# Split index query weights of all heads kept on chip; the reciprocals' table of constants replaced by an immediate

## The reference, cut to what matters

```python
iq = (hidden_states @ idx_wq_w).reshape(b, s, 16, 128)      # index queries, 16 heads
ik = hidden_states @ idx_wk_w                                # index keys, one head
iw = hidden_states @ idx_weights_w * 16 ** (-0.5)
idx_scores = einsum('bqn,bnqk->bqk', iw, relu(einsum('bqnd,bkd->bnqk', iq, ik))) * 128 ** (-0.5)
idx_scores = where(causal, idx_scores, -inf)
_, topk_idx = top_k(idx_scores, 128)
...
scores = (einsum(q_nope, k_nope) + einsum(q_pe, k_pe)) * 192 ** (-0.5)   # 32 heads
attn = softmax(where(mask, scores, -inf))
out = einsum('bhqk,bhkd->bqhd', attn, v).reshape(b, s, 32 * 128) @ o_w
```

## Time and profile before

| | us |
|---|---|
| median of 3 runs | 883.79 |
| lowest and highest | 880.57, 884.02 |
| profiled execution | 884.29 |
| its span on the core | 882.5 |

### The profile page before, as it was taken

How to read it: one execution, slowest core, us unless ns; L and a number is a source line. 1 busy time by engine, 2 the same in 40 slices (tenths; PEclk the granted TensorE clock), 3 DMA queues, 4 the chain that set the end, 5 groups by cost and what they waited for, 6 DMA issues and landing times.

```text
span 882.5 us, 20077 instructions
## 1 busy us (share of the span) xinstructions
PE 792.2 (90%) x7384; PEld 487.0 (55%) x7384; DVE 659.0 (75%) x1557; ACT 583.1 (66%) x1308; POOL 580.6 (66%) x509
## 2 busy tenths in 40 slices
PE   4979989977776998888888999999999999999998
PEld 2545544434443555555554677776766776764443
DVE  6365677889999999999988888888887888851000
ACT  2656789988886887877877677666666676750000
POOL 3175368876795788878877787887788888740000
PEclk9989999999999999999999999999999999999999
DMA  8012211112343776666676567897777677871110
GB/s 258 25 37 72 72 49 48 49 53 64 109 123 98 153 170 164 174 168 159 169 164 151 111 128 141 154 157 147 138 137 152 131 152 153 165 152 34 52 53 29
DMA packets 198483, 104.00 MB, mean 118 GB/s; under 512 B 146417, under 2 KB 172401, under 8 KB 198385
## 3 DMA queue, kind: packets, MB, share of 16 engines
q1 hardware_dynamic: 198384, 102.72, 51.9%
HBM read 36.62 MB, written 6.29 MB: 49 GB/s over the span
## 4 chain that ended last, share of the span: by engine, by line
PE 29%; POOL 26%; DVE 15%; issue 13%; DMA 7%; SPq 6%; ACT 4%; POOLq 0%; DVEq 0%; ACTq 0%
PE psS L779 9%; DMA arena<-arena 6%; DVE m L1182 4%; SPq L457 4%; PE psS L706 3%; DVE bias L1189 3%; POOL arena L1457 3%; POOL arena L1455 3%; POOL arena L1483 3%; PE psT L578 2%; PE psS L535 2%; DVE arena L1242 2%; PE psT L558 2%; POOL arena L1366 2%; POOL arena L1462 2%
## 5 line engine op out<-in xcount | busy, mean ns | idle before, releaser
L706 PE MATMUL psS<-keyT,arena 128*128 128x512 f16 (+3 forms) x1152 | 231.5, 329 | 14.9 <-DVE small L1242 6.6
L810 ACT ACTIVATE arena<-psT 128x512 f16<-128x512 f32 (+4 forms) x328 | 154.6, 503 | 110.7 <-PE psT L763 65.8
L1242 DVE CUSTOM_DVE_ANT_0 arena<-psS,bias 128x512 f32<-128x512 f32 (+7 forms) x256 | 191.4, 751 | 41.3 <-PE psS L706 17.6
L997 ACT ACTIVATE arena<-arena,small 128x512 f32<-128x512 f32 (+7 forms) x256 | 197.4, 774 | 27.7 <-DVE small L1242 21.1
L1048 DVE SCALAR_TENSOR_TENSOR arena<-psT,arena 128x512 f16<-128x512 f32 (+3 forms) x246 | 126.3, 535 | 23.1 <-ACT arena L810 22.8
L706 PEld LDWEIGHTS psS<-keyT,arena 128*128 128x128 f16 x1152 | 92.6, 98 | 81.2 <-issue 20.7
L591 PE MATMUL psS<-ikT,big 128*128 128x512 f16 (+3 forms) x528 | 103.8, 341 | 24.2 <-DVE bias L1133 20.8
L1432 POOL TENSOR_TENSOR bias<-arena,bias 128x768 f32<-128x768 f32 (+2 forms) x48 | 91.3, 1916 | 32.3 <-ACT arena L876 21.4
L763 PE MATMUL psT<-ident,arena 128*128 128x128 f32 x624 | 97.0, 277 | 10.1 <-DVE arena L1048 6.9
L591 PEld LDWEIGHTS psS<-ikT,big 128*128 128x128 f16 x528 | 49.5, 100 | 73.8 <-DVE bias L1133 28.1
L1189 DVE MATCH_REPLACE8 bias<-m,bias 128x768 f32<-128x768 f32 (+4 forms) x112 | 89.9, 809 | 0.0
(11 more groups left out here) (164 smaller groups left out, 1417.0 us busy)
## 6 DMA issues: line engine op xcount, KB each, us to landing
arena<-arena SPq DMA_DIRECT2D x192, 128.0 KB, 2.4
arena<-in_wiq SPq DMA_DIRECT2D x32, 256.0 KB, 2.8
arena<-in_ow SPq DMA_DIRECT2D x16, 512.0 KB, 4.1
arena<-in_qbT SPq DMA_DIRECT2D x16, 256.0 KB, 2.5
wvo_parts<-arena SPq DMA_DIRECT2D x16, 256.0 KB, 2.0
arena<-in_qpe SPq DMA_DIRECT2D x16, 128.0 KB, 3.0
arena<-in_x SPq DMA_DIRECT2D x8, 256.0 KB, 3.2
out<-arena SPq DMA_DIRECT2D x8, 256.0 KB, 2.0
```

Of the source, the lines that this page charges most:

```text
L706: last = mm(bank[:, k:k + w], Q[:, u % 2, h, a, q:q + P], keyT[:, b, h, k:k + w], start=(a, b) == (0, 0), stop=(a, b) == (1, 0))
L810: return nc.scalar.activation(dst, src, ACT.Copy, scale=scale)
L997: nc.scalar.activation(pr[:, g % 4, 0:kw], pr[:, g % 4, 0:kw], ACT.Exp, bias=shift[:, g % 4:g % 4 + 1], scale=-1.0, accum_out=rsum[:, unit ...
L1242: v.tensor_tensor_reduce(out=pr[:, g % 4, 0:kw], in0=bank[:, 0:kw], in1=bias[:, TOFF[t]:TOFF[t + 1]], scale=-c_s, scalar=3e38, op0=ALU.add ...
```

## The change

The split weights of all sixteen heads now have places of their own, `wqp[0]` to `wqp[15]`: in the buffers of the cosine and sine tables `cq` and `sq`, in the region of the arena that the staged query weights use later, in the two old places, and in `w1lo` and `w2s`. They are loaded and split once, in the first index loop, and the second loop reads the same. The loads of the two tables and of the first query weights wait until PE has read the places that they overwrite. In `unit_out` the table is gone: the columns that were turned by transfer get the factor 1024 as the immediate of a scalar_tensor_tensor, the others a plain product.

```diff
@@ -117,7 +117,12 @@
-        wqp = view(o + 1024, 4 * HID, F16).rearrange("p (u s k n) -> p u s k n", u=2, s=2, k=KT)
+        wq_homes = ([t[:].bitcast(F16) for t in (cq, sq)] + [view(15040, 3 * 2 * HID, F16), view(o + 1024, 4 * HID, F16)]
+                    + [t[:].rearrange("p a b -> p (a b)") for t in (w1lo, w2s)])
+        wqp = []
+        for home, slots in zip(wq_homes, (2, 2, 3, 2, 4, 3)):
+            wqp += [home[:, 1024 * j:1024 * (j + 1)].rearrange("p (s k n) -> p s k n", s=2, k=KT) for j in range(slots)]
...
@@ -367,26 +371,24 @@
+            load_iq(0, 0, True)
+            load_iq(1, 1, True)
+            for n in range(2, IH):
+                load_iq(n, n % 2, False)
+
+            sp.wait_ge(iq_mm, IH + 4)
             sp.dma_start(cq[:], cosq).then_inc(ld_cq, 16)
             sp.dma_start(sq[:], sinq).then_inc(ld_cq, 16)
-            for i in range(0, IH // 2):
-                load_iq(2 * i, 0, IH, False)
-                load_iq(2 * i + 1, 1, IH, False)
-
+            sp.wait_ge(iq_mm, IH + 7)
...
@@ -565,17 +567,18 @@
-                u, c = q % 2, q // IH
-                pe.wait_ge(wq_lo, q + 1)
+                u, (c, n) = q % 2, divmod(q, IH)
+                if not c:
+                    pe.wait_ge(wq_lo, n + 1)
                 if q >= 2:
                     pe.wait_ge(iq_lo, q - 1)
                 if c:
-                    indexer(psT[u][:], wqp[:, u], 1, iq_mm)
+                    indexer(psT[u][:], wqp[n], 1, iq_mm)
                     return
...
@@ -889,7 +892,7 @@
-                if q + 2 < 2 * IH:
+                if q + 2 < IH:
                     weights(q + 2, u, False)
...
@@ -1256,16 +1259,20 @@
                 v.reciprocal(rinv, rsum[:, u % 2, :]).then_inc(ri_done, 1)
-                dve.wait_ge(ri_done, 2 * u + 1)
-                v.tensor_tensor(rinv, rinv, scaled[:, u // NP], ALU.mult).then_inc(ri_done, 1)
                 dve.wait_ge(av_mm, UNIT_AV[u])
-                dve.wait_ge(ri_done, 2 * u + 2)
+                dve.wait_ge(ri_done, u + 1)
                 if u:
                     dve.wait_ge(ot_mm, u)
-                v.tensor_tensor(op.rearrange("p k (h r) -> p h k r", h=2),
-                                out_bank(u).rearrange("p (h k r) -> p h k r", h=2, k=4),
-                                rinv.rearrange("p (h k) -> p h k", h=2).unsqueeze(3).broadcast_to([P, 2, 4, KVR]),
-                                ALU.mult).then_inc(o_done, 1)
+                to = op.rearrange("p k (h r) -> p h k r", h=2)
+                bank = out_bank(u).rearrange("p (h k r) -> p h k r", h=2, k=4)
+                by = rinv.rearrange("p (h k) -> p h k", h=2)
+                step = 4 // len(TURNED[u // NP])
+                v.tensor_tensor(to[:, 0], bank[:, 0], by[:, 0].unsqueeze(2).broadcast_to([P, 4, KVR]), ALU.mult)
+                if step == 2:
+                    v.tensor_tensor(to[:, 1, 1::2], bank[:, 1, 1::2], by[:, 1, 1::2].unsqueeze(2).broadcast_to([P, 2, KVR]), ALU.mult)
+                v.scalar_tensor_tensor(out=to[:, 1, 0::step], in0=bank[:, 1, 0::step], scalar=PR_S,
+                                       in1=by[:, 1, 0::step].unsqueeze(2).broadcast_to([P, 4 // step, KVR]),
+                                       op0=ALU.mult, op1=ALU.mult).then_inc(o_done, 1)
...
@@ -1433,8 +1432,6 @@
             for n in range(IH):
-                if IH + n + 2 < 2 * IH:
-                    wq_parts(IH + n + 2, n % 2)
                 for g_, t in enumerate(GROUPS[1]):
```

More of the change, by code:

```diff
@@ L119, in block_kernel @@
         wq32 = view(o, 2 * HID).rearrange("p (u k n) -> p u k n", u=2, k=KT)
-        wqp = view(o + 1024, 4 * HID, F16).rearrange("p (u s k n) -> p u s k n", u=2, s=2, k=KT)
+        wq_homes = ([t[:].bitcast(F16) for t in (cq, sq)] + [view(15040, 3 * 2 * HID, F16), view(o + 1024, 4 * HID, F16)]
[3 more added lines that the diff above has]
+            wqp += [home[:, 1024 * j:1024 * (j + 1)].rearrange("p (s k n) -> p s k n", s=2, k=KT) for j in range(slots)]
+        assert len(wqp) == IH
         wikp = keyT[:, 0, 0, :].rearrange("p (s k n) -> p s k n", s=2, k=KT)
@@ L180, in block_kernel @@
         eps_t = small[:, 400:401]
-        scaled = small[:, 408:424].rearrange("p (c s) -> p c s", c=2)
         nmax_s = small[:, 424:428]
@@ L210, in block_kernel @@
         sq_done = sem("sq_done"); n_sqrt = sem("n_sqrt")
-        rsn_done = sem("rsn_done"); eps_ok = sem("eps_ok"); ones_ok = sem("ones_ok")
+        rsn_done = sem("rsn_done"); eps_ok = sem("eps_ok")
         g_sub = sem("g_sub"); g_exp = sem("g_exp"); gw_done = sem("gw_done")
@@ L369, in _, with load_iq @@
             sp.dma_start(bm32, bm).then_inc(ld_c, 16)
+            wiq_v = wiq.rearrange("(k p) n -> p k n", p=P)
+            def load_iq(n, u, first):
+                if not first:
+                    sp.wait_ge(wq_lo, n - 1)
+                sp.dma_start(wq32[:, u], wiq_v[:, :, ds(n * ID, ID)]).then_inc(ld_wq[u], 16)
+            load_iq(0, 0, True)
[3 more added lines that the diff above has]
+            sp.wait_ge(iq_mm, IH + 4)
             sp.dma_start(cq[:], cosq).then_inc(ld_cq, 16)
             sp.dma_start(sq[:], sinq).then_inc(ld_cq, 16)
-            wiq_v = wiq.rearrange("(k p) n -> p k n", p=P)
-            def load_iq(n, u, again, first):
-                if not first:
-                    sp.wait_ge(wq_lo, n + again - 1)
-                sp.dma_start(wq32[:, u], wiq_v[:, :, ds(n * ID, ID)]).then_inc(ld_wq[u], 16)
-            load_iq(0, 0, 0, True)
-            load_iq(1, 1, 0, True)
-            for i in range(1, IH // 2):
-                load_iq(2 * i, 0, 0, False)
-                load_iq(2 * i + 1, 1, 0, False)
-            for i in range(0, IH // 2):
-                load_iq(2 * i, 0, IH, False)
-                load_iq(2 * i + 1, 1, IH, False)
+            sp.wait_ge(iq_mm, IH + 7)
             def load_qw(p, u, first):
@@ L577, in iq_head @@
                     for a, b in ((0, 0), (0, 1), (1, 0)):
-                        last = mm(psT[u][:, 0:CH - P], wqp[:, u, a, k, :], xnT[:, b, k, P:CH],
+                        last = mm(psT[u][:, 0:CH - P], wqp[n][:, a, k, :], xnT[:, b, k, P:CH],
                                   start=ins == 0, stop=ins == 3 * KT - 1)
@@ L858, in weights @@
                 act.wait_ge(ld_wq[u], 16 if first else 8 * (q - u) + 16)
-                copy(wqp[:, u, 0], wq32[:, u], W_S).then_inc(wq_hi, 1)
+                copy(wqp[q][:, 0], wq32[:, u], W_S).then_inc(wq_hi, 1)
                 copy(wq32[:, u], wq32[:, u], W_S).then_inc(wq_hi, 1)
@@ L1305, in _ @@
                 row_max(g)
-            dve.wait_ge(eps_ok, 2)
             for g in range(STEPS):
@@ L1347, in _ @@
             g.memset(eps_t, EPS).then_inc(eps_ok, 1)
-            g.memset(small[:, 408:424], 1.0).then_inc(ones_ok, 1)
-            pool.wait_ge(ones_ok, 1)
-            for c in range(2):
-                for s in TURNED[c]:
-                    at = col_of(s)
-                    ins = g.memset(scaled[:, c, at:at + 1], PR_S)
-            ins.then_inc(eps_ok, 1)
             g.memset(bias[:], 0.0).then_inc(idx_init, 1)
@@ L1365, in wq_parts @@
                 pool.wait_ge(wq_hi, 2 * q + 2)
-                g.tensor_tensor(wqp[:, u, 1], wq32[:, u], wqp[:, u, 0], ALU.subtract).then_inc(wq_lo, 1)
+                g.tensor_tensor(wqp[q][:, 1], wq32[:, u], wqp[q][:, 0], ALU.subtract).then_inc(wq_lo, 1)
             pn = [0]
@@ L1421, in _ @@
             gated_rows()
-            for q in range(6, IH + 2):
+            for q in range(6, IH):
                 wq_parts(q, q % 2)
```

## The result

| kernel | median us | lowest and highest | runs |
|---|---|---|---|
| before | 882.60 | 880.57, 884.02 | 4 |
| changed | 873.04 | 871.21, 874.62 | 4 |

The ratio is 0.9888, with a 95% interval of 0.9851 to 0.9926: by it 9.9 us less, between 6.5 and 13.2 (the medians lie 9.6 apart). Forecast were 874.2 us and 9.8 less, with a range of 870.5 to 878.5. The profiled execution of the changed kernel took 871.21 us, the fastest of its four, with a span of 869.4.

What follows compares the result with a forecast made beforehand. A chain of waits over several engines was taken to bound the second index loop, with PE next. The loop's 9.2 us and the reciprocals' 0.6 made 9.8 less: 874.2 us forecast, range 870.5 to 878.5.

Steps and rivals of the forecast that it cites:

- The sum for the loop: Second index loop, 14 passes: PE alone at 4.39 or 4.82 us per pass, 65.8 us instead of 75.2, 9.4 less.
- the 0.2 held back for DVE: Second index loop: 9.2 us taken instead of 9.4, since 0.2 may go where DVE splits the values in one pass.
- A chain of waits over several engines: Second index loop before the change: no engine full, so waits across engines set the pace, 5.37 us per pass.
- The shift: Behind the index loop: masks, POOL's last additions and DVE's selection loop move with the last projection, by the same amount.
- The loads and memsets: Later table and query-weight loads, and POOL's seven small memsets gone from the start: no cost or gain.
- The term of the reciprocals: Ends of low attention units on DVE: 0.12 us less each, 1.8 at most over 15, a third counted: 0.6 less.
- The two readings of a split: Low unit ends: by trace distances 0.12 us less each; by the skill's rule added instructions cost 0.25, no gain.
- The hand-overs stay: Second index loop: passes with transposes stay near 5.1 us, loop 6.6 less, kernel 877; chance 0.12.
- A slower low half: Low attention: added DVE latency (4.5 us) and clock falls (25) lose 30 against 9.2 won, kernel 904; chance 0.03.
- their latency: Low attention: added DVE instructions cost their whole latency, 4.5 us more, clock as before, kernel 879; chance 0.06.
- The gain stays in the loop: Index loop to selection: DVE's selection is behind PE, only 4 of the 9.2 us arrive, kernel 880; chance 0.07.
- It does more: Loop and low half: 9.4, all 1.8 of the low units and 1.7 from clock falls, 13 less, 871; chance 0.08.

## Why the prediction was right, step by step

- **The sum for the loop held.** Worked out 65.8 us, measured 65.74 or 65.75 in every kernel that keeps the weights and leaves PE's work, ACT's work and PE's waits alone. Of the two ends, 7.1 from the busy column and 9.4 from the starts, the starts were right (9.47), and the 0.2 held back for DVE wasn't needed. The tail of about 0.17 us on 14 runs of matmuls is the whole difference between 68.11 and 65.75.
- **What held the loop was told too coarsely.** "A chain of waits over several engines" was right, and named were the copies ahead of the relu and the subtraction behind the additions. It came out as two mechanisms: the ring through POOL's order (6.7 us alone) and ACT's load in passes with transposes (2.4 alone), 10.2 together. POOL's 15 us less of work were worth nothing by themselves. The 16 loads aren't needed to explain the 75.22, though no run put them back alone.
- **The shift reached the end.** All that follows the loop moved by the same 10.28 us (190.36 for 200.64; "near 191"). DVE was no second bound.
- **The loads and memsets cost nothing**, as said: DVE is busy 75.02 us of the first 76.36 of the selection loop (75.03 before), and no wait for them appears.
- **The term of the reciprocals was too small.** Forecast 0.6 us, being a third of 15 x 0.12. The term is mis-sized in two steps. The wait for the reciprocal is 0.29 us and not 0.26, so that a unit gains 0.09 instead of 0.12 and takes 1.03 us there and not "within 1.0". And counting only a third of it was wrong: in the first six periods all of it arrives, and 15 x 0.09 = 1.3. The sum 9.5 + 1.3 would have been 10.8, or 873.
- **How near the total came is in part luck.** 9.8 were forecast, and 9.9 measured within 6.5 to 13.2. The two later measurements of the same change gave 12.8 (ratio 0.9855) and 11.9 (0.9866), so that the forecast of the gain is rather 1 to 3 us low. The reciprocals account for 0.7 of that; the rest is within what the clock does from execution to execution, and isn't pinned down.
- **The two readings of a split.** The prediction weighed its own 0.20 and 0.34 from start to start against a rule that would have made the added pieces cost 0.25. Two that follow at once stand 0.13 us apart with 64 columns, 0.20 with 128 and 0.34 with 256. The Trainium skill (VectorE: DVE Perf Modes, the section on the TRN2 errata) has 120 cycles at 0.96 GHz, 0.125 us, for an instruction that reads PSUM, and adds its columns; by that I estimate 0.19 us for 64 and 0.26 for 128. The durations here come near it (0.21, 0.28), the distances don't; a row of small pieces costs by its distances. The section gives its advice to keep pieces at 512 elements for the latency of SBUF, and these pieces come out of PSUM, so that it bears less on this split than the prediction had it.
- **The rivals.** "The hand-overs stay" (5.1 a pass) didn't happen: 4.82. It is what the loop does when ACT's copies are put back, 5.13. "A slower low half" and "their latency" didn't: the units got shorter. "The gain stays in the loop" didn't either. "It does more" came true in part: its 1.8 for the low units was 1.3, and in the profile with 871.21 us the low half has no period under a clock of 1.00 (the 1.5 us of idle time that the prediction read as one gap in the earlier trace rows are two, of 0.7 and 1.1 us, the first of which begins ahead of that window). Another such stretch has come up in the last stage:

```profile
796.00:804.00 8.00, 5.99 (x22) 2.30 (x21) 1.89 (x3) 0.60 (x1) 0.00 (x0) 0.79 0.40 131
```

Such stretches come and go between executions of one kernel. The prediction was right to leave them out of its sum and to give them to the range.

## What to carry to other kernels

When no engine of a loop is full, look for an instruction that the bound engine waits for and ask what stands ahead of it in its own engine's order: here a 1.2-us subtraction cost 6.7 us for standing behind two additions, and nothing at all once nobody waited for it. To price the loop without it, add up start-to-start distances of the engine that will be the bound, not busy times, and check that the next fullest engine stays under that per pass. And where one engine is over 90% busy, as DVE was in the low half, ask first whether a small saving on it arrives in full: here 0.09 us a unit did, in the units that could be compared.

## What the runs showed of the hardware

- Pieces that DVE reads from PSUM back to back cost about 0.07 us each on top of their columns, far less than one shown duration: 0.13, 0.20 and 0.34 us apart for 64, 128 and 256 columns, while their durations are 0.21, 0.28 and 0.42.
- In this kernel 0.01 less of mean granted clock goes with 4.1 +- 0.6 us more of 872, over 23 executions. An execution at 0.996 and one at 0.984 of the same kernel (871.87 and 875.79 us) lie 3.9 apart, four tenths of what the change brings.
- Neither 14 more subtractions on POOL (15 us of work) nor their reads and writes in SBUF slowed PE, ACT or DVE in that loop: it took 65.74 against 65.75 us, with ACT busy 55.92 against 56.13 and DVE 57.89 against 57.75.
- Small instructions of DVE can be long: in the changed kernel's gates a copy of 16 columns took 0.97 us and an addition of 8 columns 1.01, each beside POOL's large products, where a reciprocal of 8 columns took 0.20.

```profile
57.05 0.97 DVE L1154 COPY grep<-small 128x16 f32<-128x16 f32 x1
...
60.69 1.01 DVE L1160 TENSOR_TENSOR small<-small 128x8 f32<-128x8 f32 x1
61.73 0.20 DVE L1161 RECIPROCAL small<-small 128x8 f32<-128x8 f32 x1
```

Each of the long ones ends within 0.05 us of the end of an instruction of POOL (58.02, 60.39 with a comparison of 64 columns that took 1.05, and 61.70; POOL's end at 58.00, 60.35 and 61.66), and the same three do so in the kernel before (58.84, 61.20, 62.49; POOL's 58.81, 61.15, 62.47). Other small instructions of DVE beside POOL's products aren't long, as the reciprocal shows, so that this points at POOL and doesn't show what it is of POOL's that holds them up.
